# A two-layer adaLN transformer kernel: layer norm of the first batch before the constants, halves of 512 tokens in the first and last unit, a new plan of the order

## What is computed

```python
mod = (_silu(L0_c) @ L0_wmod).reshape(8, 6, 1, -1)     # sa, ca, ga, sb, cb, gb
ga = (2 * (ga >= 0) - 1) * jnp.maximum(jnp.abs(ga), 0.25)      # gb likewise
h = _layernorm(x) * (1 + ca) + sa
x = x + ga * attention0(h)          # 16 heads of 16, causal, ALiBi, softmax, projection + bias
h = _layernorm(x) * (1 + cb) + sb
x = x + gb * (sigmoid(xr @ W_r) * (square(relu(xk @ W_k)) @ W_v))   # xr, xk: mixed with the token before
# layer 1: the same frame; attention1 with RoPE, and as feed-forward one linear map
x = x + gb * (h @ (W + up_aux @ (lora_up @ (lora_down @ down_aux))).T + b)
```

## Time and profile before

| what | value |
|---|---|
| median of 3 runs (lowest, highest) | 2933.96 us (2933.64, 2935.0) |
| the profiled execution's own time | 2937.21 us |
| its span, first to last instruction | 2935.4 us |
| mean granted clock of TensorE, share of full speed | 0.933 |
| busy: PE, DVE, ACT, POOL | 85%, 80%, 58%, 29% |

### The profile page before, as it was taken

The page is one execution under the profiler, slowest core; times in us unless marked ns, Lnnn a source line. Parts: engine busy times, 40 slices in busy tenths (PEclk is TensorE's granted clock), DMA queues, the critical chain, the costliest instruction groups (busy, mean ns, idle before and its releaser), DMA issues.

```text
span 2935.4 us, 54933 instructions
## 1 busy us (share of the span) xinstructions
PE 2480.4 (85%) x18968; PEld 1070.4 (36%) x18968; DVE 2340.0 (80%) x7126; ACT 1716.9 (58%) x3458; POOL 850.4 (29%) x954
## 2 busy tenths in 40 slices
PE   5688888988888987988989889798897988988786
PEld 3323433432334333343343334343333433433323
DVE  4598768789887898868988788887888789876793
ACT  2267565556564666556656566665665556656474
POOL 3111341234221342224222252222512234225121
PEclk8789999999999999989999899899998989999898
DMA  5611142113312223212223113231222212301200
GB/s 171 193 38 37 35 123 85 58 46 88 102 41 92 66 66 96 75 61 64 74 88 105 46 48 105 70 93 46 76 88 75 77 64 80 97 28 59 87 14 15
DMA packets 142393, 218.29 MB, mean 74 GB/s; under 512 B 21190, under 2 KB 62556, under 8 KB 142052
## 3 DMA queue, kind: packets, MB, share of 16 engines
q1 hardware_dynamic: 142120, 214.77, 23.7%
HBM read 137.87 MB, written 77.89 MB: 74 GB/s over the span
## 4 chain that ended last, share of the span: by engine, by line
PE 53%; DVE 33%; ACT 6%; issue 4%; DMA 1%; SPq 1%; POOL 0%; DVEq 0%; ACTq 0%; POOLq 0%
PE ctx_ps L1501 12%; DVE small L1269 11%; PE big L1426 10%; PE small L1460 9%; PE big L1482 8%; PE big L1415 7%; DVE mx L1267 5%; PE big L1531 4%; ACT probs L1049 3%; DVE stats L1218 3%; PE big L1515 2%; DVE mx L1269 2%; DVE region L1328 2%; ACT xn L1098 1%; DVE ctx_b L1298 1%
## 5 line engine op out<-in xcount | busy, mean ns | idle before, releaser
L1049 ACT ACTIVATE probs<-big 128x512 f32<-128x512 f32 (+2 forms) x2560 | 1222.9, 565 | 499.6 <-PE big L1482 493.5
L1269 DVE CUSTOM_DVE_ANT_0 small<-small,mask 128x128 f32<-128x128 f32 (+3 forms) x2048 | 941.5, 520 | 107.8 <-PE small L1460 99.6
L1267 DVE TENSOR_REDUCE mx<-small 128x1 f32<-128x512 f32 x1024 | 651.0, 684 | 190.2 <-PE small L1460 183.3
L1482 PE MATMUL big<-stack_q,stack_k 64*128 64x512 f16 (+3 forms) x6144 | 700.0, 332 | 99.7 <-ACT probs L1049 62.8
L961 POOL TENSOR_SCALAR_AFFINE_SELECT probs<-probs 128x512 f32<-128x512 f32 x512 | 331.9, 655 | 1364.4 <-ACT probs L1049 1363.5
L1460 PE MATMUL small<-stack_k,stack_q 64*128 64x512 f16 (+3 forms) x3072 | 473.3, 346 | 237.6 <-DVE mx L1269 154.2
L1501 PE MATMUL ctx_ps<-probs,v_ones 128*17 128x512 f32 (+3 forms) x6144 | 617.9, 499 | 4.1 <-POOL probs L961 3.8
L1460 PEld LDWEIGHTS small<-stack_k,stack_q 64*128 64x128 f16 x3072 | 123.6, 95 | 804.5 <-DVE mx L1269 416.1
L1482 PEld LDWEIGHTS big<-stack_q,stack_k 64*128 64x128 f16 x6144 | 259.5, 95 | 428.9 <-issue 218.0
L1269 DVE DVE_READ_ACCUMULATOR2_ANT mx<- 128x1 f32 x2048 | 285.7, 140 | 0.0
L1415 PE MATMUL big<-hT,w_qkv 128*128 128x512 f32 x512 | 269.0, 637 | 16.4 <-DMA w_qkv<-wqkv 13.4
(11 more groups left out here) (91 smaller groups left out, 1958.6 us busy)
## 6 DMA issues: line engine op xcount, KB each, us to landing
image<-region SPq DMA_DIRECT2D x192, 256.0 KB
stack_q<-image SPq DMA_DIRECT2D x64, 512.0 KB, 3.6
stack_k<-image SPq DMA_DIRECT2D x64, 512.0 KB, 4.6
lo_dram<-region SPq DMA_DIRECT2D x64, 256.0 KB
w_qkv<-wqkv SPq DMA_DIRECT2D x16, 768.0 KB, 4.8
x_res<-x SPq DMA_DIRECT2D x32, 256.0 KB, 5.0
stack_q<-lo_dram SPq DMA_DIRECT2D x128, 64.0 KB, 3.9
stack_k<-lo_dram SPq DMA_DIRECT2D x128, 64.0 KB, 4.6
```

Source lines behind the costliest of these rows:

```text
L1049: s.activation(probs[:, n % HELD, heads, q0:], big[:, at.slot(turn), 0:len(pairs) * width] .rearrange("p (h q) -> p h q", h=len(pairs)), A ...
L1267: last = v.reduce_max(to, held, AX)
L1269: last = v.tensor_tensor_reduce(out=held, in0=held, in1=mask[:, BANK - width:], scale=1.0, scalar=3.0 * NEG, op0=ALU.add, op1=ALU.max, acc ...
L1482: last = te.matmul(big[:, at.slot(at.turn() + parity), j * width:(j + 1) * width], stack_k[rows, c, g * PAIR_N + pair, kt * P:(kt + 1) * P ...
```

## The change

**Start.** The loads of the ten constants are taken apart. `c` comes first, then `x` of batch 0, layer 0's modulation weights (`mods_in`), `w_qkv`, the fixed rows, `x` of batch 1, the other constants (`once_in`) and `x` of batch 2. No engine waits for all constants at its head. What unit 0 needs of the modulations is an item `mods` ahead of its first transposes; the rest (LoRA product, gates, layer 1's modulations) are four items `once` between the turns of value and ahead of the first max step. The write of gates and product and `post_loads` come behind the first `stack_load`.

**Halves.** `layernorm_items` takes tiles `a` to `b`. Unit 0's first layer norm and the last unit's second one run as two halves of 4 tiles (512 tokens), each with a chain of its own and transposes behind it. The last unit's blocks go in the order (g,blk) = (0,0), (1,0), (0,1), (2,0), (1,1), (3,0), (2,1), (3,1), and its first two projection turns, layer norm of 4 tiles, bias, transposes, linear map and store can come when block 0 of all groups is done. In every unit after the first the copy to `modc` stands behind the chain.

**Plan.** New constants; work on DVE is put into the list only when its input is ready now (`CHAIN_EASE` 0); the price has terms for a DVE left idle behind proj and y, and for DVE or ACT without input.

```diff
-LN_STEPS = 33
+LN_CHAIN = 17
+def in_parts(unit, which):
+    return (unit, which) in ((0, 0), (N_UNITS - 1, 1))
+def attention_blocks(unit):
+    if unit < N_UNITS - 1:
+        return [(g, blk) for g in range(NG) for blk in range(BLOCKS)]
+    first, second = [(g, 0) for g in range(NG)], [(g, 1) for g in range(NG)]
+    return [first[0], *(x for n in range(1, NG) for x in (first[n], second[n - 1])), second[-1]]
+def layernorm_items(unit, which, a=0, b=NT):
+    return [("ln", unit, which, phase, n, a, b) for phase, n_from, n_to in (("stats", a, b), ("chain", 0, LN_CHAIN), ("xn", a, b))
+            for n in range(n_from, n_to)]
+def normed_and_turned(unit, which):
+    if in_parts(unit, which):
+        return [i for tb in range(2) for i in layernorm_items(unit, which, 4 * tb, 4 * tb + 4) + turned(unit, which, tb)]
+    return layernorm_items(unit, which) + turned(unit, which)
 def post_sequence(unit):
-    if layer == 0:
+    if in_parts(unit, 1):
+        for tb in range(2):
+            a, b = 2 * tb, 2 * tb + 1
+            out += [("proj", unit, a), ("proj", unit, b)] + layernorm_items(unit, 1, 4 * tb, 4 * tb + 4)
+            out += [("bias", unit, a), ("bias", unit, b)] + turned(unit, 1, tb)
+            out += [i for n in (a, b) for i in (("y", unit, n), ("y_add", unit, n), ("store", unit, n))]
+    elif layer == 0:
-QK_LAGS = (0.0, 0.5000, 1.6000, 2.0000, 5.9576)
+QK_LAGS = (0.0, 0.7758, 1.7394, 3.0788, 5.9576)
-PULL = {"score": 0.0400, "context": 0.0246, "max": 0.0424, "pre": 0.0400, "post": 0.0561}
-AHEAD = {"score": 0.0143, "context": 0.0100, "max": 0.8411, "pre": 1.1458, "post": 0.0079}
+PULL = {"score": 0.0400, "context": 0.0165, "max": 0.0483, "pre": 0.0191, "post": 0.0472}
+AHEAD = {"score": 0.0124, "context": 0.0085, "max": 0.7639, "pre": 1.5711, "post": 0.0063}
-SEEN, DMA_NS = 251.9964, 495.7496
-ROWS_FIRST = 334.5784
+SEEN, DMA_NS = 232.7037, 466.9094
+CHAIN_EASE, IDLE = 0.0000, 0.0465
+FEED = {"DVE": 0.0101, "ACT": 0.1761}
+ROWS_FIRST = 576.2205
+def ease(engine):
+    return CHAIN_EASE if engine == "DVE" else EASE
...
         def price(option):
+            if item[0] in ("proj", "y"):
+                end = max(model.free["PE"], model.needs(item)) + pe_time(item)
+                cost += IDLE * max(0.0, end + SEEN - model.free["DVE"])
+            begin = max(model.free["PE"], model.needs(item)) + (TURN_COST if model.shape_of(item) != model.shape else 0.0)
+            for engine, feeder in (("DVE", "max"), ("ACT", "score")):
+                if feeder in feeders:
+                    fed = begin + pe_time(item) + (0.0 if name == feeder else FIRST_FEED[feeder]) + SEEN
+                    cost += FEED[engine] * max(0.0, fed - max(model.free[engine], model.free["PE"]))
...
+def with_start(items):
+    out = [("x_load", 0, n) for n in range(4)] + [("mods_in", 0), ("pre_loads", 0), ("fixed_rows", 0)]
+    out += [("x_load", 1, n) for n in range(4)] + [("once_in", 0)] + [("x_load", 2, n) for n in range(4)]
+    before = {("turned", 0, 0, 0, 0): [("mods", 0)], ("value", 0, 0, 0): [("once", 0, 0)], ("value", 0, 0, 1): [("once", 0, 1)],
+              ("value", 0, 1, 0): [("once", 0, 2)], max_stream(0)[0]: [("once", 0, 3)]}
+    after = {("stack_load", 0, 0): [("spill", 0), ("post_loads", 0)]}
...
-            pool.wait_ge(consts_in, 16 * n_consts)
-            act.wait_ge(consts_in, 16 * n_consts)
+            act.wait_ge(c_in, 32)
-            dve.wait_ge(consts_in, 16 * n_consts)
+            dve.wait_ge(c_in, 32)
-            pe.wait_ge(consts_in, 16 * n_consts)
...
+                if kind == "mods":
+                    pe.wait_ge(silu_done, 3)
+                    pe.wait_ge(mods_in, 16)
+                    modulations(0).then_inc(mods_mm, 1)
+                    gates_of(0, ctx_ps[0:B])
```

More of the change, by code:

```diff
@@ L397, in barred @@
         if kind == "proj":
-            return ("norm", unit, NG - 1, BLOCKS - 1, 3) not in seen
+            return ("norm", unit, NG - 1, item[2] // 2 if in_parts(unit, 1) else BLOCKS - 1, 3) not in seen
         if name == "post" and kind == "turned":
@@ L401, in barred @@
         if kind in ("scale", "bias"):
-            return unit and ("post_loads", unit) not in seen or open_("pre", unit, "ln")
+            return (("post_loads", unit) if unit else ("stack_load", 0, 0)) not in seen or open_("pre", unit, "ln")
         return False
@@ L415, in follow @@
                     ready, engine = model.other_needs(queue[0])
-                    if ready > max(now, model.free[engine]) + EASE:
+                    if ready > max(now, model.free[engine]) + ease(engine):
                         break
@@ L428, in follow @@
                     blocked = True
-                if not blocked and ready() <= max(now, model.free[engine]) + EASE:
+                if not blocked and ready() <= max(now, model.free[engine]) + ease(engine):
                     emit(item)
@@ L499, in plan @@
         done = sum(taken.values()) / whole
+        feeders = [n for n, i in options if n in FIRST_FEED and model.needs(i) < model.free["PE"] + FEED_WAIT]
         def price(option):
@@ L542 @@
 MODEL = Model()
-ITEMS = [("x_load", 0, n) for n in range(4)] + [("pre_loads", 0), ("spill", 0), ("post_loads", 0)]
-ITEMS += [("x_load", b, n) for b in range(1, STREAMS) for n in range(4)]
-ITEMS += plan(MODEL)
+PLAN = plan(MODEL)
+def with_start(items):
[4 more added lines that the diff above has]
+    after = {("stack_load", 0, 0): [("spill", 0), ("post_loads", 0)]}
+    seen = set()
+    for item in items:
+        own = item[2] if item[0] == "half" else item
+        if own not in seen:
+            out += before.get(own, [])
+        seen.add(own)
+        out += [item] + after.get(item, [])
+    return out
+ITEMS = with_start(PLAN)
 TURN_KINDS = ("score", "rows", "proj", "turned", "gate", "key", "y", "qk", "value")
@@ L561, in events @@
         e[f"stack_{item[2]}"] = 1
-    if kind == "ln" and item[3] == LN_STEPS - 1:
+    if ln_ends(item):
         e["normed"] = 1
+    if kind == "mods" or kind == "ln" and item[3:6] == ("chain", LN_CHAIN - 1, 0) and item[1:3] != (0, 0):
+        e["modulated"] = 1
     if kind == "norm" and item[4] == 3:
@@ L1247, in layernorm, with modulate @@
                 else:
-                    mark(v.tensor_tensor(rstd[:], rstd[:], tmp[:], ALU.mult))
+                    mark(v.tensor_tensor(rstd_, rstd_, tmp_, ALU.mult))
+            def modulate(at, unit, which):
+                batch, layer = UNITS[unit]
+                if unit:
+                    wait_all_emptied(dve, at, [at.turns[i] for i in turned(unit - 1, which)])
+                cols = modT[:, 8 * layer:8 * layer + 8, batch:batch + 1]
+                v.tensor_copy(modc[:, which], cols.rearrange("p k o -> p (k o)")).then_inc(modc_ready, 1)
@@ L1336, in step @@
                     add = bank.rearrange("p (t n) -> p t n", t=2)
-                    if layer and n == 0:
-                        dve.wait_ge(biased, at.now("bias"))
+                    if layer:
+                        dve.wait_ge(biased, at.nth["bias", unit, n])
                     wait_filled(dve, at)
@@ L1507, in step @@
                         pe.wait_ge(scaled, at.now("scale"))
+                    if first and (item[2] == 0 or in_parts(unit, 1)):
                         pe.wait_ge(ctx_ready, at.now("ctx_ready"))
@@ L1544, in step @@
                         pe.wait_ge(scaled, at.now("scale"))
-                        if layer:
-                            wait_h(at, unit, 1)
-                        else:
+                        if not layer:
                             pe.wait_ge(squared, at.now("square"))
+                    if item[2] % 2 == 0 and first and layer:
+                        wait_h(at, unit, 1, item[2] // 2)
                     token_turn(at, h_all if layer else k_act, w_ffn[:, 2], item[2], first, second)
```

334 lines of the change are left out of this document (188 added, 146 removed).

## The result

The changed kernel takes 2813.12 us (median of 4 runs, 2811.8 to 2815.85), the kernel before beside it 2933.8 (4 runs, 2924.58 to 2935.0): a ratio of 0.9589 with a 95% interval of 0.9574 to 0.9605. The profiled execution took 2814.14 us, its span is 2812.1, its mean clock 0.951.

A forecast was written before the change was run, and what follows sets the result against it. No engine was full; a latency chain at start and end, PE and DVE sharing the middle's pace. Start -27, middle -15, end 0 gave -42 from 2937.2: 2895, or 2892 for the median; range 2875 to 2908, 8 in 10 2866 to 2924.

The forecast's parts named there:

- The start: Up to the first max step: earlier `x`, weights and saves bring that step at 75.4, 27 us earlier (bounds 21 and 30).
- The middle: Between start and end: ease 0 lays chain links between max steps, 15 us less (bounds nothing and 25).
- The 45 us of DVE and 15 of time: Layer norm chains: 448 links x 0.10 us of DVE come free, counted at a third of the pace.
- Rival 2: Middle: the plan gives more, feeding takes a twelfth of PE's idle time; 2861 us (2850 to 2868), chance 0.08.
- Spread links and POOL: Chain links beside POOL's splits: 55 us lost now, 58 when spread, so nothing was added.
- rival 4: Chain links: slower, as spread links meet POOL, 270 instead of 60 of 448; 2970 us, chance 0.06.
- The end: Behind the last maxima: halves save 13.7 us behind the last context, 23 more lie behind the maxima; taken as 0.
- +9: End: the total if PE's 16 us freed ahead of the last maxima are worth nothing, as DVE sets the pace.
- -7: End: the total if PE's 16 us freed ahead of the last maxima are filled with attention of unit (6,1).
- bounds of -14 and +10: End: the range given around the 0, with what spare there is in PE's 32 us (10 us idle).
- Rival 3: Whole kernel: first max step earlier, but unit 1 late next, all meets at the same place; 2928 to 2940, chance 0.05.
- Rival 1: Whole kernel: head start arrives, plan gives nothing, end costs 10; 2917 us (2905 to 2927), chance 0.20.

The follow-up runs named there:

- e8: Kernel before with ease 0 for layer norm items on DVE alone, plus one wait on POOL: 2960.91 us, ratio 1.0107.
- e15: Kernel before with all of the new `PULL` and `AHEAD` and nothing else but one wait on POOL: 2853.62 us, ratio 0.9729.
- e12: Kernel before with the new PULL, AHEAD, SEEN, DMA_NS, ROWS_FIRST and QK_LAGS, old ease, no price terms, one wait on POOL: 2860.04 us, ratio 0.9754.
- e2: Kernel before (old start, wholes) with all planner constants and price terms of the change, ease 0 and one wait on POOL: 2822.98 us, ratio 0.9624.
- e5: Changed kernel without the price terms (`IDLE` and both `FEED` weights at 0): 2867.43 us, ratio 0.9782.
- e3: Changed kernel with the old ease for DVE (`CHAIN_EASE` 500.5758): 2870.77 us, ratio 0.9781.
- e9: Changed kernel with the old `PULL` and `AHEAD` alone: 2964.1 us, ratio 1.0107.
- e6: Changed kernel with the old PULL, AHEAD, SEEN, DMA_NS, ROWS_FIRST and QK_LAGS, keeping ease 0 and the price terms: 2939.95 us, ratio 1.0027.
- e1: Changed kernel with the plan's old constants, old ease and no idle or feed terms (new start and halves alone): 2930.61 us, ratio 0.999.
- e17: Changed kernel with the lead of pre alone (`AHEAD`) set back to 1.1458: 3021.96 us, ratio 1.0297.
- e4: Changed kernel with the last unit in wholes, g by g, and the first unit still in halves: 2795.72 us, ratio 0.9518.
- e16: Changed kernel with both the first and the last unit in wholes, new start otherwise kept: 2790.13 us, ratio 0.9519.
- e11: Changed kernel with PULL of four queues moved by 2 to 3 per cent and `SEEN` 237, a meaningless nudge: 2836.53 us, ratio 0.9671.

## Why the prediction was wrong

**The start (-27, measured -23.3).** The mechanism and the size are right. The weights landed at 12.4 (11 taken), q and k started at 27.95 (27), saves at 37.5 (36.6), the first stack load at 61.6 (61.9). The miss is in the last step, 79.05 for 75.4. From the first stack load to the first max step I took the 11.5 us of before; it is 17.5. In both kernels 16 matmuls of unit 1's q and k stand ahead of the first max step. Before, they waited for their weights until 93.6, 2.7 us behind the stack load; after, unit 1's transposes wait for its `xn` until 67.1, and so these matmuls start at 70.9, 9.4 us behind the load. The sum had no term for unit 1's layer norm, which the new start puts behind the `once` items.

**The middle (-15, measured -125.3 in ten units). This is the step that failed:** "what I can price is `CHAIN_EASE`", with bounds of 0 and 25. The price was near for that one edit where DVE and PE are full. The 45 us of DVE and 15 of time were for the whole kernel, so 28 and 9 for ten units; e8 gave 49 and 14.7 there, 53 us of DVE in all, and time at 0.30 of it, as the third that was taken. Its cover was not right: in the first and last units the stacks come late (the last unit's first load lies 77 us behind the last rows ahead of it, before 18), and by itself the edit makes the kernel 27 us slower. What I left at nothing carried the gain. The weights of the queues alone are worth 80 us on the kernel before (e15), and ease 0 with the price terms 37 more on the new constants (e12 to e2): together the plan's 111, within the draw. Taken back from after, each part costs more than its share: the price terms 54 (e5), the ease of DVE 58 (e3), the weights 151 (e9). On the old constants ease and price terms give nothing (e6 against e1), and there the stacks come 4 us behind the last rows and not 46 ahead. Rival 2, "the plan gives more", had the sign and the place, and took a twelfth of PE's idle time where 37% of it went (86 of 234 us in ten units). The right bound stood in the earlier trace rows: PE idle 382 us and DVE 476 in the middle, with the durations of the work fixed. A new order can take any part of that, so on the side of the gain it could have been bounded by it. On the other side the idle time is no bound; e17 lost 209 us to after by one number.

**Spread links and POOL (nothing, measured nothing after).** 0.289 us a link against 0.293. Of 476 links 96 lasted over 0.3 us beside a POOL instruction, 0.79 in the mean; before 74 of 448 and 0.92 (60 were estimated). The meetings are somewhat more and cost less each, far from the 270 of rival 4.

**The end (0, measured +15.4).** The terms were near: 28.4 us behind the last context (25.1 forecast, before 38.8), 50.9 between the first scores behind the last rows and it (48 forecast, before 25.0). The step at fault is the choice of 0 between +9 and -7: I let the PE time that is freed ahead of the last maxima be half used. e4 shows that it is not: PE stands 13.7 us there, against 5.3 with wholes, and the last rows come no earlier. +9 with the terms' own errors (+3 each) is the +15.4, which lies outside the bounds of -14 and +10. Halves at both ends cost some 20 us (e16, 23 by the medians).

**Rivals.** Rival 3, no change, is what start and halves give without the plan (e1, 0.999), though not as I put it: the head start reached the last rows and was lost behind them. Rival 1 was nearest at the end (+10) and had the plan wrong.

**Shown and open.** Shown: the gain lies in the ten full units, as less waiting of PE and DVE for each other; the weights carry some 80 of the plan's 111 us; the lead of pre is what keeps the stacks in time; start and halves cancel under the old plan, and under the new one the start brings what it was forecast to and the halves take most of that back. The clock is granted at 0.98 instead of 0.94 where PE waits less, and the max matmuls took 343 and 334 ns, so some of the 39 us of busy time may be the clock's; how much was not taken apart. Open: which of the weights of context, max and post does it (only pre was taken apart), by which steps of the order they shorten the waits, what ease 0 does for DVE's other work, and how much below 25 us of any term is the draw of the plan (e11).

## What to carry to other kernels

A change of a planner's weights is not bounded by the one edit that can be priced. Bound its gain by the idle time of the two engines that share the pace, give its loss room of the same size or more, and allow for it to be the largest term. Before a setting back is read as what a part was worth, look whether it broke something else: here it made the stacks late. Work moved behind the last wait costs its full length unless something is named that will fill the hole it leaves in front; cutting the last unit in halves hid 10 us behind the last context and put 26 ahead of it. When single constants are tested, run a meaningless nudge beside them first: here it moved the time by 23 us, and a gain below that can't be put down to a constant.

## What the hardware showed

- A DVE operation on 128x4 elements (`ve<-mv`) that takes 0.17 us at 21.70, with POOL idle, took 3.18, from 9.53 to 12.71, beside POOL's MEMSET of `stack_k` (5.76 to 12.68), and ended with it. In e16 the same line on 128x8 started at 11.30 and took 1.42, to the end of the same MEMSET. Four BATCH_NORM_STATS2 in the same time (7.68, 1.40 for all) were not held up. The first agrees with the Trainium skill, page "SBUF — State Buffer", section "SBUF: two separate sides", by which the one of DVE and GpSimd that starts first holds their shared ports for its whole instruction.
- 32 matmuls of the modulations took 6.97 us at the start of the span, 0.22 each, where 64 took 9.62 before, 0.15 each. The windows give a clock of 1.00 for the first and 0.74 for the second, so the recorded clock does not explain it; what does is open.
- The same matmuls of the max steps took 343 ns at a granted clock of 0.94 and 334 at 0.98, in stretches of ten units that differ in PE's idle time (234 and 148 us). The records there are at full or at half clock, half for 212 us before and 79 after. In the other runs the clock of that stretch goes with PE's idle time too (0.94 with 268 us in e17, 0.96 with 177 in e15, 0.98 with 149 in e2). That the waits set it fits these runs and was not tested by itself.
